# In slots 0 to 5 of the first two attention layers, output products and rope are listed ahead of the norm of the batch two ahead, instead of mixed with it

## What is computed

```
# layer 0: 16 heads of 32, 4 key heads, sparse mask
h = layernorm(x) * (1 + scale) + shift
q = h @ Wq.T;  c = h @ Wkd.T;  k = c @ Wku.T;  v = c @ Wvu.T
q, k = rope(q), rope(k)
x = x + softmax(mask(q k^T / sqrt(32))) v @ Wo.T
# layer 1: 8 heads of 64, 1 key head, no mask
h = rmsnorm(x) * (w * (1 + scale))
q, k, v = h @ Wq.T, h @ Wk.T, h @ Wv.T;  q, k = rope(q), rope(k)
x = x + softmax(q k^T / 8) v @ Wo.T
x = x + (silu(h2 @ Wg.T) * (h2 @ Wu.T)) @ Wd.T      # h2: second rmsnorm
# layer 2: attention and MLP; layer 3: experts, norm, output product
```

## Time and profile before

| | |
|---|---|
| median of 3 runs | 2400.38 us (2399.41 to 2405.69) |
| profiled execution | 2398.59 us |
| its span | 2396.8 us |
| slots 0 to 5, in the span | about 94 to 617 us |
| TensorE busy | 2244.7 us, 94% |
| VectorE, ScalarE, GpSimd busy | 1168.9, 1033.6, 292.5 us |

### The profile page before, as it was taken

How to read it: one execution, slowest core, us unless ns; L and a number is a source line. 1 busy time by engine, 2 the same in 40 slices (tenths; PEclk the granted TensorE clock), 3 DMA queues, 4 the chain that set the end, 5 groups by cost and what they waited for, 6 DMA issues and landing times.

```text
span 2396.8 us, 34593 instructions
## 1 busy us (share of the span) xinstructions
PE 2244.7 (94%) x14034; PEld 1511.1 (63%) x14034; DVE 1168.9 (49%) x2499; ACT 1033.6 (43%) x2425; POOL 292.5 (12%) x246
## 2 busy tenths in 40 slices
PE   5889999999999999999999989999999989999998
PEld 2455555555555687888877756565664668888633
DVE  2345454454457344433443356657587554544322
ACT  2355555444446221111113366657676552222473
POOL 3331122122021001110001010101010110000021
PEclk9889999999999999999999999999999999999999
DMA  8310020000010002110102211011110101100001
GB/s 274 113 40 27 15 64 26 23 23 18 18 40 27 31 27 84 54 61 27 36 6 79 79 53 67 31 63 36 54 36 19 53 1 36 36 1 1 1 18 53
DMA packets 59487, 104.97 MB, mean 44 GB/s; under 512 B 10592, under 2 KB 24560, under 8 KB 59328
## 3 DMA queue, kind: packets, MB, share of 16 engines
q1 hardware_dynamic: 58368, 100.30, 12.6%
q0 software_dynamic: 960, 2.45, 0.3%
HBM read 77.04 MB, written 10.49 MB: 37 GB/s over the span
## 4 chain that ended last, share of the span: by engine, by line
PE 84%; ACT 7%; DVE 6%; POOL 1%; issue 1%; SPq 1%; DMA 1%; DVEq 0%; POOLq 0%; ACTq 0%
PE banks L1213 36%; PE banks L404 22%; PE banks L740 6%; PE banks L732 4%; PE banks L756 4%; ACT sb_Pr L842 2%; PE banks L766 2%; PE banks L265 1%; ACT sb_PT L847 1%; PE banks L906 1%; DVE sb_hN L364 1%; PE banks L630 1%; PE banks L638 1%; DVE sb_Pr L812 1%; PE banks L890 1%
## 5 line engine op out<-in xcount | busy, mean ns | idle before, releaser
L1213 PE MATMUL banks<-sb_HH,sb_Ws 128*128 128x512 f32 x1536 | 490.2, 392 | 12.7 <-DVE sb_HL L1103 7.3
L1213 PEld LDWEIGHTS banks<-sb_HH,sb_Ws 128*128 128x128 f32 x1536 | 289.6, 189 | 76.7 <-issue 16.7
L1213 PE MATMUL banks<-sb_hidH,sb_Ws 128*128 128x512 f32 x1024 | 331.2, 392 | 0.4 <-DVE sb_x L1284 0.4
L842 ACT ACTIVATE sb_Pr<-sb_Pr,sb_nmax 128x512 f32<-128x512 f32 (+4 forms) x512 | 291.6, 576 | 30.9 <-DVE sb_nmax L812 30.8
L1213 PE MATMUL banks<-sb_HL,sb_Ws 128*128 128x512 f32 x768 | 300.0, 391 | 0.0
L847 ACT ACTIVATE sb_PT<-banks 128x512 f32<-128x512 f32 (+2 forms) x320 | 143.5, 496 | 302.6 <-PE banks L740 225.5
L740 PEld LDWEIGHTS banks<-sb_ident,sb_Pr 128*128 128x128 f32 x1536 | 169.7, 142 | 125.5 <-issue 38.9
L819 DVE COPY sb_PT<-banks 128x512 f32<-128x512 f32 (+2 forms) x320 | 168.6, 563 | 163.1 <-PE banks L740 108.7
L740 PE MATMUL banks<-sb_ident,sb_Pr 128*128 128x128 f32 x1536 | 214.2, 282 | 18.2 <-DVE sb_A L830 5.0
L1213 PEld LDWEIGHTS banks<-sb_hidH,sb_Ws 128*128 128x128 f32 x1024 | 192.3, 188 | 44.0 <-issue 2.5
L1213 PE MATMUL banks<-sb_hidL,sb_Ws 128*128 128x512 f32 x512 | 199.4, 389 | 0.0
(11 more groups left out here) (160 smaller groups left out, 3251.7 us busy)
## 6 DMA issues: line engine op xcount, KB each, us to landing
sb_ring<-split_units SPq DMA_DIRECT2D x48, 512.0 KB, 3.3
sb_ropet<-sb_R SPq DMA_DIRECT2D x70, 128.0 KB, 2.0
sb_staged<-in_L_cond_Wfc SPq DMA_DIRECT2D x16, 512.0 KB, 4.6
sb_wada<-in_L_cond_Wada SPq DMA_DIRECT2D x6, 1024.0 KB, 5.5
split_units<-sb_unitpair SPq DMA_DIRECT2D x12, 512.0 KB, 2.9
sb_x<-in_x SPq DMA_DIRECT2D x4, 1024.0 KB, 9.1
sb_staged<-in_L_cond_Wg SPq DMA_DIRECT2D x8, 512.0 KB, 3.7
sb_staged<-in_L_cond_Wu SPq DMA_DIRECT2D x8, 512.0 KB, 4.7
```

Source lines behind the costliest of these rows:

```text
L842: ins = e.activation(prob, prob if s.biased else k.bank(n % 4)[:, 0:s.width(u)], ACT.Exp, bias=s.stat(k, k.nmax, b, u), scale=-1.0 if s.bi ...
L1213: mm = e.matmul(bank, lhsT, rhs, start=i == 0, stop=i == len(mats) - 1)
```

## The change

Only the last two members of the merge change places. The norm of the batch two ahead leaves the merge and stands by itself behind it. Nothing is added or removed, and each slot has as many beats as before, at the same places.

```diff
         for m in range(2 * B - 1):
             late = beats(posts[m - 1]) if m else []
-            sides01.append(([] if m else pre(1, 0)) + pre(m + 1, 1) + among(late, pre(m + 1, 2), pre(m + 2, 0)) + [[]])
+            sides01.append(([] if m else pre(1, 0)) + pre(m + 1, 1) + among(late, pre(m + 1, 2)) + pre(m + 2, 0) + [[]])
```

## The result

The changed kernel takes 2419.57 us (median of 4 runs, 2418.47 to 2420.06) against 2399.89 us before. The ratio is 1.0078, with a 95% interval of 1.0063 to 1.0093. It is 0.8% slower, where 2420 us had been forecast.

A forecast was written before the change was run, and what follows sets the result against it. It took TensorE, busy 94% of the span, as the bound, with single waits deciding. Slot terms 10 + 4 + 3 + 2 + 1 = 20 us on 2398.59 gave 2418.6, forecast as 2420 since that execution lay 1.8 under the median; range 2406 to 2434.

The forecast's parts named there:

- Slot 0: Slot 0: longer wait for swap 2's DMA, then waits at sin 4 and the mean product; about 10 us, bounds 5 and 14.
- The mean product: Slot 0: TensorE's mean product waits for GpSimd's sums behind add 4; 3.5 of 4.4 us charged, bounds 0 and 4.4.
- The wait at sin 4: Slot 0: VectorE waits 2.5 us at sin 4 for swap 4; 1.5 us charged to TensorE, bounds 0 and 2.5.
- The two idle times behind the mean product: Slot 0: TensorE's 1.68 and 0.74 us behind the burst of centrings and squares, uncovered before and now, cost the same.
- its upper bound: Slot 0: bound of 14 us, said to have room for the granted clock at its lower level of 1.2 GHz.
- Slot 1: Slot 1: sin 2's wait mostly covered (0.5), uncovered norm burst (+2.0), three closer norm waits (1.5); 4 us, bounds 1 to 7.
- the sign given for being right: Slot 1: an idle time of 2 to 3 us behind the mean product would show the forecast right.
- the 3.7 us worked out: Slot 1: VectorE would wait 3.7 us at sin 2, covered by the third output product; 0.5 us charged.
- Slot 2: Slot 2, norm of layer 1: four squares now uncovered (+2) and a closer chain behind (+1); 3 us, bounds 0.5 to 6.
- The rival that it evens out: Slot 0 leaves 5 us, slots 1 to 5 bursts 2 to 3, slot ends give back some 5; about 2403 us, chance 0.13.
- Slots 3 to 5: Slot 3: squares' idle time only partly new, 2 us (0 to 4); slots 4 and 5: bursts vanish, 1 us for both (0 to 3).
- The faster rival: Ends of layer 0's slots lose their idle times and clock dip, -10.0 us; 2390 if slot 0 costs nothing besides; chance 0.07.

The follow-up runs named there:

- Apart_sums_earlier: Changed kernel with the norm's sums over x one beat earlier, ahead of the last rope beat, in slots 0 and 1; ratio 1.0046 to the kernel before.
- apart_covered: Changed kernel with sums over x one beat earlier in slots 0 and 1, slot 1's last output product directly behind the mean product; ratio 1.0035 to the kernel before.
- mixed_repeats_last: Kernel before, with SyncE's swaps 2 to 4 of layer 0 issued ahead of the 15 repeat DMAs; ratio 0.9970 to the kernel before.

## Why the prediction was right

**Slot 0: the places were right, the size by a balance.** Counted from the landmark, which is 1.0 us late, add 0 ends at 148.3; it had ended at 151.9, so it is 3.6 us earlier (forecast 3.4). Sin 2 starts at 161.8 (forecast 162.4), VectorE waits 11.4 us (forecast 11 to 12), and TensorE's turn comes 11.7 us later than before (forecast 12.3). The mean product waits 3.58 us (3.5 charged). The whole is 9.4 us for 10. But the 10 us were all priced as idle time, and idle time grew by only 5.2. The wait at sin 4 is 1.0 us and holds TensorE up by nothing that can be seen, where 1.5 had been charged. The two idle times behind the mean product (1.68 and 0.74 us), forecast to stay, don't show in the slow stretch. The other 4.2 us are work at the lower clock, which the forecast had left to its upper bound.

**Slot 1: the term was too small, 7.7 us for 4, and outside its bounds of 1 to 7.** The mean product waits for the sums, and sin 2's wait (0.78 us) is covered by the output product, as forecast. But the sign given for being right, an idle time of 2 to 3 us behind the mean product, did not come: the long wait of 2.40 us is in front of it, and 0.76 us are behind. What failed above all is the price. The term counted idle time alone and kept the clock for slot 0's upper bound; idle time grew by 1.0 us and slow work by 6.7. Apart_sums_earlier and apart_covered show where: taking away the wait of 2.4 us won 3.8, and a product behind the burst won 2.8 with no idle time saved. Sin 2 also met a shorter wait than the 3.7 us worked out: from the end of add 0 at 234.4 swap 2 took 14.5 us.

**Slot 2: the term was too large, 0.0 us for 3, and under its bounds.** The squares do cost something at their new place, 1.27 us. The end of the slot gives most of it back: the idle time of 1.58 us is 0.53 now. In sum idle time is 1.0 us shorter and slow work 0.9 us longer. The rival that it evens out had named the gain at the end, and here it holds. TensorE of the changed kernel:

```profile
361.69 0.41 PE L906 MATMUL banks<-sb_ident,sb_Pr 128*128 128x128 f32 x2 [1.27 <-ACT sb_PT L847]
...
372.70 1.33 PE L890 MATMUL banks<-sb_R 32*128 32x128 f32 x8 [0.53 <-DVE sb_nmax L812]
```

**Slots 3 to 5: right in number**, 1.9 us for 2 and 0.3 for 1, **and in slot 3 for another reason.** The 2 us were to be idle time behind the squares. That wait is 2.17 us at 443.88, for 2.45 before, and idle time in the stretch fell by 0.9 us. What grew is slow work, by 2.7 us: the windows from 440 to 460 are at 0.74, where before one window at the wait, from 390 to 400, is at 0.83 and the next at 1.00.

So the sum was right to a microsecond by luck, twice over. The errors of slots 1 and 2 (+3.7 and -3.0) cancelled. And the 20 us had been added up from idle times, while the traces show 4.4 us of idle time and 14.9 us of slow work. The forecast had the waits in the right places for the most part, but not the rule by which they cost time. The faster rival would have needed slot 0 to cost under 3 us. It falls, though its premise holds in one slot. The rule of the Trainium skill cited ahead (Perfetto Trace Analysis, section Optimization Strategy), that interleaving may help, agrees with the result as a whole, and in slot 1 one output product put back behind the mean product brought 2.8 us.

## What to carry to other kernels

Before moving an instruction that waits for a DMA, measure the latency from what releases the transfer to where its data are used. Then count how much work will stand between the two, and look at what else is in the DMA queue ahead of it. Here a reorder of the compute lists stretched TensorE's wait behind that latency from 7.01 to 11.67 us, and a reorder of the queue alone won 7 us for the whole kernel. When two orders are compared with a bottleneck taken away, take it away from both: the repaired order matched the old kernel, and yet was 7 us behind the old order with the same repair. Split a loss into idle time and slow work before explaining it. A wait on TensorE costs more than itself where the clock is seen to fall behind it, and a piece of TensorE's own work behind a burst can keep the clock up (2.8 us here) even where it saves no idle time.

## What the runs showed of the hardware that was not expected

The granted clock falls behind some short idle times and not behind others. Behind 2.40 us at 268.33 in the changed kernel it was 0.50 for the next window, with TensorE busy for 9.19 of 10 us in it. Behind 1.97 us at 271.14 in the kernel before it stayed at 1.00. In mixed_repeats_last the same wait of 1.97 us comes at the same place of slot 1, at 260.75, and there the window from 260 to 270 is at 0.83. What makes the difference was not found.

Most of what a reorder cost here was not waiting. Of 19.3 us, 14.9 were the same matmuls done at a lower granted clock.
